# Two of eight maxima pairs per key strip through the score banks, reduced by VectorE in one instruction for both tiles

## The chip, the cores and the metric

The kernel runs on one core of a Trainium2 chip. The metric is the device time of one execution in microseconds; the times of a kernel are compared by the median of their runs. TensorE (PE) multiplies matrices into PSUM, which has eight banks of 128 partitions x 512 fp32; VectorE (DVE) and ScalarE (ACT) read them.

## The reference

Two transformer layers on 4,096 tokens of 256 features with 16 heads of 16. The first has block-sparse causal attention and an fp8 product. The second has two dense causal attentions over all 4,096 tokens, one with rotary positions and one with normalised queries and keys and a mixture of experts behind it. The dense attentions are what this case is about:

```
scores = jnp.einsum('bhqd,bhkd->bhqk', Q, K) / math.sqrt(Dh)
scores = jnp.where(causal, scores, jnp.finfo(scores.dtype).min)
attn = jax.nn.softmax(scores, axis=-1)
y = jnp.einsum('bhqk,bhkd->bhqd', attn, V)
```

## The kernel before

`attend` runs first for the sparse attention (stage "sparse") and then for both dense ones (stage "dense"). In the dense stage a unit is one strip j of 512 queries of a group of four heads; there are 2 attentions x 4 groups x 8 strips = 64 units. The strips go up from 0 to 7 in one group and down in the next. A unit has 4(j + 1) chunks of 128 keys, the last four of them on the diagonal, so that all have 1,152 chunks.

Softmax needs the maximum of each query over its keys before the exponentials. The kernel makes the scores twice. Ahead of time, with queries on the partitions, it makes a **tile** for each key strip kc, head h and block b of 128 queries: one product of 128 x 512 into one of three side banks (PSUM banks 5 to 7), of which VectorE takes the maximum into a column of `maxes`. That is 16 tiles per key strip, 4 per chunk, 4,608 in all. Tiles of the diagonal key strip (kc == j) are 128 to 512 columns wide and go through a masked reduction (L944), the others through a plain one (L951). When a unit's tiles are done VectorE negates the maxima ("negate"), TensorE transposes them ("hand", L818), and a DMA puts them into extra rows of the queries.

Later, with keys on the partitions, comes the **score**: for each chunk two pairs of products (L845), two heads into two neighbouring banks (pair 0 in banks 0 and 1, pair 1 in banks 2 and 3). ScalarE turns each pair into probabilities with one exp over 128 x 1,024 (L908), and the next user of the pair's banks waits for that exp. One chunk later TensorE **weighs** the values with them (L885, four heads side by side into bank 4; each product stands as two records in the trace). At a unit's end ScalarE copies bank 4 (L913), and in the second chunk of the next unit TensorE transposes the copy ("out", L823) into a side bank, and VectorE divides.

Heads with even and odd numbers use the upper and lower half of TensorE's rows, so that two such products run side by side. Only order on each engine and semaphores set the schedule. The order is written out in `order`: tiles go ahead of the scores by `lead(n)` chunks, and `emit_tiles(goal)` puts tiles into the order until their number reaches the goal. Before, a chunk reads on TensorE: two tiles, two score pairs, two tiles, the weighing of the chunk before. A side bank's next user waits for VectorE's reduction of the third tile back.

In short signs, used below: T a tile, S a score pair, W a weighing, "wide" the new pair.

## Time and profile before

| what | value |
| --- | --- |
| median of 3 runs | 5092.77 us (5092.59 to 5112.78) |
| span of the profiled execution | 5116.3 us |
| PE, DVE, ACT busy over the span | 4781.3, 4006.1, 2867.2 us |
| PE busy share over the span | 93% |
| dense stage | about 1179 to 4360 us |
| mean granted TensorE clock | 0.934 |

The profiled execution is one execution of its own, and its span lies just above the highest of the three runs; no time of its own is given beside the span. A group's busy time is the union of its instructions, and the ends of matmuls are modelled. Start times of matmuls are more telling than their lengths.

### The profile page before, as it was taken

The page shows a single profiled execution, that of the slowest core. Times are in us where ns is not written, and L with a number is a line of the kernel's source. Part 1 is how long each engine was busy: PE and PEld are TensorE (multiplying, and loading weights), DVE is VectorE, ACT ScalarE, POOL GpSimd, SP SyncE. Part 2 cuts the span into 40 slices and gives each one's busy share as a digit, 9 for nine tenths or more (in the row PEclk, how much of TensorE's full clock was granted, in tenths as well). Part 3 has the DMA queues.
Part 4 walks back from the last instruction along what each step waited for, and adds up shares of the span by engine and source line. Part 5 has one row for each costly group of instructions (what it writes and reads, how often), then busy time and mean ns, then how long its engine had stood idle before and what let it go on. Part 6 is the DMA issues. An engine that isn't in the chain of part 4 may idle for free.

```text
span 5116.3 us, 82733 instructions
## 1 busy us (share of the span) xinstructions
PE 4781.3 (93%) x31872; PEld 2539.4 (50%) x31872; DVE 4006.1 (78%) x9075; ACT 2867.2 (56%) x3349; POOL 241.8 (5%) x259
## 2 busy tenths in 40 slices
PE   6699997868999999999999999999999999899999
PEld 5455555754434344433334433334443333688888
DVE  8677775767898988888888989988899875555555
ACT  4356554433566766666666667666567677332232
POOL 5200001110000000000000000000000000300000
PEclk9799898877899999999999999999899999899999
DMA  6622223765000201200300300300300000210010
GB/s 192 175 77 69 65 51 105 230 221 97 16 11 14 48 16 32 43 9 5 50 13 21 58 9 5 50 13 20 54 11 8 9 7 7 71 42 21 21 42 9
DMA packets 259185, 258.36 MB, mean 50 GB/s; under 512 B 78288, under 2 KB 198096, under 8 KB 257440
## 3 DMA queue, kind: packets, MB, share of 16 engines
q1 hardware_dynamic: 250784, 212.86, 14.8%
q0 software_dynamic: 6240, 38.80, 4.7%
q8 instruction: 251, 4.11, 0.3%
q10 hardware_dynamic: 1768, 1.42, 0.2%
q14 instruction: 142, 1.16, 0.1%
HBM read 145.44 MB, written 105.97 MB: 49 GB/s over the span
## 4 chain that ended last, share of the span: by engine, by line
PE 73%; DVE 19%; issue 5%; ACT 2%; SPq 1%; DMA 1%; DVEq 0%; ACTq 0%
PE psum L885 24%; PE psum L813 20%; PE psum L76 14%; DVE maxes_dense L951 11%; PE psum L845 4%; PE psum L777 3%; PE psum L802 2%; PE psum L823 1%; PE psum L854 1%; PE psum L1656 1%; DVE masked_scores_dense L944 1%; PE psum L809 1%; PE psum L1636 0%; PE psum L864 0%; ACT probs_dense L908 0%
## 5 line engine op out<-in xcount | busy, mean ns | idle before, releaser
L908 ACT ACTIVATE probs_dense<-psum 128x1024 f32<-128x1024 f32 (+3 forms) x2304 | 2068.1, 950 | 1042.2 <-PE psum L845 755.1
L951 DVE TENSOR_REDUCE maxes_dense<-psum 128x1 f32<-128x512 f32 x3584 | 2227.5, 684 | 232.1 <-PE psum L813 231.3
L813 PE MATMUL psum<-keys,queries_dense 48*128 48x512 f32 (+3 forms) x4608 | 1553.0, 477 | 114.6 <-DVE maxes_dense L951 22.1
L813 PEld LDWEIGHTS psum<-keys,queries_dense 48*128 48x128 f32 x4608 | 668.2, 191 | 1471.4 <-DVE maxes_dense L951 1143.6
L885 PE MATMUL psum<-probs_dense,values 128*32 128x512 f32 (+3 forms) x9216 | 1181.2, 591 | 0.0
L845 PE MATMUL psum<-queries_dense,keys 50*128 50x512 f32 (+3 forms) x4608 | 809.7, 407 | 11.5 <-ACT probs_dense L908 11.2
L944 DVE CUSTOM_DVE_ANT_0 masked_scores_dense<-psum,causal_add 128x128 f32<-128x128 f32 (+3 forms) x1024 | 452.4, 488 | 151.5 <-PE psum L813 132.2
L845 PEld LDWEIGHTS psum<-queries_dense,keys 50*128 50x128 f32 x4608 | 449.6, 193 | 106.4 <-ACT probs_dense L908 60.0
L944 DVE CUSTOM_DVE_ANT_0 masked_scores_sparse<-psum,after_add 128x512 f32<-128x512 f32 x512 | 326.2, 687 | 99.9 <-PE psum L802 99.0
L1763 ACT ACTIVATE activated<-psum 128x512 f32<-128x512 f32 x208 | 124.4, 598 | 417.5 <-PE psum L76 405.8
L885 PEld LDWEIGHTS psum<-probs_dense,values 128*32 128x32 f32 x9216 | 189.9, 109 | 273.1 <-issue 203.0
L908 ACT ACTIVATE probs_sparse<-psum 128x1024 f32<-128x1024 f32 x224 | 217.7, 1022 | 147.2 <-PE psum L777 59.7
L802 PE MATMUL psum<-str_keys,queries_sparse 48*128 48x512 f32 x512 | 179.6, 513 | 48.3 <-DMA own_values<-v_scratch 25.8
L1898 DVE CAST hid_high<-activated 128x512 fp32r<-128x512 f32 x208 | 91.9, 442 | 143.5 <-ACT activated L1763 140.7
L1900 DVE TENSOR_TENSOR hid_low<-activated,hid_high 128x512 fp32r<-128x512 f32 x208 | 150.4, 723 | 7.2
L802 PEld LDWEIGHTS psum<-str_keys,queries_sparse 48*128 48x128 f32 x512 | 72.2, 195 | 168.2 <-DVE maxes_sparse L944 88.8
L885 PE MATMUL psum<-probs_sparse,str_values 128*32 128x512 f32 x1024 | 148.7, 655 | 0.0
L777 PE MATMUL psum<-tri_key,eye_bf 64*128 64x128 bf16 x2048 | 147.3, 223 | 0.0
L908 ACT ACTIVATE probs_sparse<-psum,after_bias 128x1024 f32<-128x1024 f32 x96 | 101.6, 1111 | 67.0 <-PE psum L854 67.0
L854 PE MATMUL psum<-queries_sparse,str_keys 50*128 50x512 f32 x512 | 127.3, 462 | 1.6 <-ACT probs_sparse L908 1.6
L948 DVE TENSOR_REDUCE maxes_sparse<-psum 128x4 f32<-128x512 f32 x128 | 83.7, 689 | 53.3 <-PE psum L809 51.7
L1912 DVE SCALAR_TENSOR_TENSOR xa_s<-psum,wts,xa_s 128x192 f32<-128x192 f32 x128 | 52.8, 416 | 81.6 <-PE psum L76 80.8
(296 smaller groups left out, 5252.6 us busy)
## 6 DMA issues: line engine op xcount, KB each, us to landing
v_scratch<-ve_s SPq DMA_DIRECT2D x96, 256.0 KB, 3.5
queries_dense<-parts_scratch SPq DMA_DIRECT2D x384, 64.0 KB
keys<-parts_scratch POOLq DMA_DIRECT2D x42, 512.0 KB, 18.0
parts_scratch<-part_high SPq DMA_DIRECT2D x16, 1024.0 KB, 4.3
parts_scratch<-part_low SPq DMA_DIRECT2D x16, 1024.0 KB, 7.1
values<-v_scratch POOLq DMA_DIRECT2D x8, 2048.0 KB, 35.3
queries_sparse<-parts_scratch SPq DMA_DIRECT2D x192, 64.0 KB
own_keys<-parts_scratch SPq DMA_DIRECT2D x192, 64.0 KB
```

The source lines that it names most:

```text
L76: m = pe.matmul(out_ap, left(l, c), right(r, c), start=(n == 0), stop=(n == len(pairs) - 1))
L777: m = pe.matmul(bank, eye2[own, part, :], addend, start=start and part == 0, stop=stop and part == 1)
L802: m = pe.matmul(bank, q[rows(h, TROWS), h // 2, b * P:(b + 1) * P], str_keys[n // STRIPS][rows(h, TROWS), h // 2, :], start=True, stop=True)
L813: m = pe.matmul(bank[:, 0:width], q[rows(h, TROWS), h // 2, b * P:(b + 1) * P], k[rows(h, TROWS), h // 2, kc * STRIP:kc * STRIP + width], ...
L845: m = pe.matmul(full[:, first_col:STRIP], k[own, h // 2, c * P:(c + 1) * P], q[own, h // 2, first_col:STRIP], start=True, stop=not diagonal)
L854: m = pe.matmul(full, str_keys[n // STRIPS][own, h // 2, c * P:(c + 1) * P], q[own, h // 2, :], start=True, stop=not partly)
L885: m = pe.matmul(psum[own_rows, 4, cols], vt, probs[(2 * m_at + h // 2) % 6][:, h % 2, cols], start=(c == 0), stop=(c == sizes[n] - 1 and b ...
L908: act.activation(probs[i % 6][:, :, first_col:STRIP], psum[:, at2:at2 + 2, first_col:STRIP], ACT.Exp, scale=SCALE, **extra).then_inc(exp_d ...
L944: m = dve.tensor_tensor_reduce(out=masked_scores[e % 2][:, 0:width], in0=bank[:, 0:width], in1=mask, scale=1.0, scalar=-3e38, op0=ALU.add, ...
L951: m = dve.tensor_reduce(mx[:, h * BLOCKS + b, kc:kc + 1], bank, AX.X, ALU.max)
L1763: act.activation(gs[k % 2][:], h_bank(u), func).then_inc(activated, 1)
L1900: dve.tensor_tensor(low[:, f, :], g[:], high[:, f, :].bitcast(F32), ALU.subtract).then_inc(hid_split, 1)
```

## The change

Of the eight pairs of tiles (even and odd head, same block of queries) that a full key strip has, the two of the last block of queries (b = 3, one for each pair of heads) no longer go to side banks. They become one **wide** pair: TensorE writes both tiles into the pair of score banks whose turn it is (L851 in the new kernel), and VectorE takes the maxima of both in one instruction over 128 x 2 x 512. So each key strip below the diagonal keeps 12 tiles and gets 2 wide pairs; the strip on the diagonal keeps 16 tiles. There are 448 wide pairs in place of 896 tiles.

Score pairs and wide pairs now take the two pair banks in turn, in the order in which they stand (`pair_users`, `wait_pair`). Each waits for the user two before it: for its exp if it was a score pair, for VectorE's wide reduction if it was a wide pair.

The tiles are spread over two chunks: an even chunk has S S T T W, an odd one T S wide T T T S W. Where there is no wide pair in the piece (the diagonal strip's tiles), the odd chunk has T S T T T T T S W. The leads are rounded to even numbers of chunks.

Counted in the new order, its 576 pairs of chunks are: 283 with a wide pair and nothing else, 60 with a wide pair in which the unit's own scores are on the diagonal, 33 more with a wide pair and a "hand", 50 with a wide pair at the start of a unit ("out"), 7 with a burst of tiles at a unit's end, 125 with tiles of the diagonal strip, 18 without tiles.

The core of the diff:

```diff
@@ -573,33 +573,44 @@
             if sparse:
                 return [("strided", 2 * i + odd, b) for i in range(PAIRS) for b in range(BLOCKS) for odd in range(2)] + [
                     ("local", odd, b) for b in range(0, BLOCKS, 2) for odd in range(2)]
-            return [(kc, 2 * i + odd, b) for kc in range(j + 1) for i in range(PAIRS) for b in range(BLOCKS) for odd in range(2)]
+            return [(kc, 2 * i + odd, b) for kc in range(j + 1) for i in range(PAIRS) for b in range(BLOCKS) for odd in range(2)
+                    if kc == j or b < BLOCKS - 1]
+
+        def steps_of(n):
+
+            steps = [("tile", n, tile) for tile in tiles_of(n)]
+            if sparse:
+                return steps
+            for kc in reversed(range(units[n][2])):
+                for i in reversed(range(PAIRS)):
+                    steps.insert(kc * GROUP * (BLOCKS - 1) + i * 2 * (BLOCKS - 1) + 3, ("wide", n, (kc, i, BLOCKS - 1)))
+            return steps
 
         def lead(n):
             if sparse:
                 return sizes[0] + 2
             if n >= len(units) - STRIPS:
                 return sizes[n] + 4
-            return min(max(sizes) + 4, 10 + int((2 * BLOCKS * (ends[n] - sizes[n])) ** 0.5))
+            return min(max(sizes) + 4, 2 * int(5 + (2 * BLOCKS * (ends[n] - sizes[n])) ** 0.5 / 2))
 
         order = []
-        ahead = [(n, t) for n in range(len(units)) for t in tiles_of(n)]
-        at = 0
+        ahead = [step for n in range(len(units)) for step in steps_of(n)]
+        at = made = 0
 
         def emit_tiles(goal):
-            nonlocal at
-            while at < min(goal, len(ahead)):
-                n, tile = ahead[at]
-                first_tile = at == 0 or ahead[at - 1][0] != n
-                if first_tile:
+            nonlocal at, made
+            while at < len(ahead) and made < goal:
+                kind, n, what = ahead[at]
+                if at == 0 or ahead[at - 1][1] != n:
                     order.append(("queries", n + 1, None))
-                order.append(("tile", n, tile))
-                of_unit = at - 4 * (ends[n] - sizes[n])
-                if of_unit == 5 and n >= 1:
+                order.append((kind, n, what))
+                before, made = made, made + (2 if kind == "wide" else 1)
+                of_unit = 4 * (ends[n] - sizes[n]) + 5
+                if before <= of_unit < made and n >= 1:
                     order.append(("hand", n - 1, None))
                 at += 1
-                if at == 4 * ends[n]:
+                if made == 4 * ends[n]:
                     order.append(("negate", n, None))
                     if n == len(units) - 1:
                         order.append(("hand", n, None))
@@ -610,17 +621,29 @@
             order.append(("unit", n, None))
             for c in range(sizes[n]):
                 m = ends[n] - sizes[n] + c
-                emit_tiles(4 * (m + lead(n)) + 2)
+                goals = [4 * (m + lead(n)) + more for more in (2, 2, 4)]
+                if not sparse:
+                    goals = [4 * (m - c % 2 + lead(n)) + more for more in ((0, 0, 2), (3, 8, 8))[c % 2]]
+                emit_tiles(goals[0])
                 for h in range(GROUP):
                     order.append(("score", n, (m, c, h)))
                     if n >= 1 and c == 1 and h == 3:
                         order.append(("out", n - 1, None))
                     if h % 2 == 1:
-                        emit_tiles(4 * (m + lead(n)) + (2, 4)[h // 2])
+                        emit_tiles(goals[1 + h // 2])
                 if c >= 1:
                     order.append(("weigh", n, (m - 1, c - 1)))
             order.append(("weigh", n, (m, c)))
         order.append(("out", len(units) - 1, None))
+
+        pair_users, wide_at = [], {}
+        for kind, n, what in order:
+            if kind == "wide":
+                wide_at[n, what] = len(wide_at)
+                pair_users.append(("reduced", wide_at[n, what] + 1))
+            elif kind == "score" and what[2] % 2 == 1:
+                pair_users.append(("exp_done", 2 * what[0] + what[2] // 2 + 1))
+        ring_at = {user: r for r, user in enumerate(pair_users)}
 
         side_at = {}
@@ -777,10 +801,16 @@
                             m = pe.matmul(bank, eye2[own, part, :], addend, start=start and part == 0, stop=stop and part == 1)
                     return m
 
+                def wait_pair(r):
+
+                    if r >= 2:
+                        name, count = pair_users[r - 2]
+                        pe.wait_ge(wide_reduced if name == "reduced" else exp_done, count)
+
                 if sparse:
                     pe.wait_ge(sparse_masks_in, SPARSE_MASKS)
                 for kind, n, what in order:
-                    if kind not in ("tile", "hand", "out", "unit", "score", "weigh"):
+                    if kind not in ("tile", "wide", "hand", "out", "unit", "score", "weigh"):
                         continue
                     a, g, j = units[n]
                     slot = n % held if sparse else n // STRIPS % 2
@@ -813,6 +843,14 @@
                             m = pe.matmul(bank[:, 0:width], q[rows(h, TROWS), h // 2, b * P:(b + 1) * P],
                                           k[rows(h, TROWS), h // 2, kc * STRIP:kc * STRIP + width], start=True, stop=True)
                         m.then_inc(side_filled, 1)
+                    elif kind == "wide":
+                        kc, i, b = what
+                        r = ring_at["reduced", wide_at[n, what] + 1]
+                        wait_pair(r)
+                        for odd in range(2):
+                            m = pe.matmul(psum[:, 2 * (r % 2) + odd, :], q[rows(odd, TROWS), i, b * P:(b + 1) * P],
+                                          k[rows(odd, TROWS), i, kc * STRIP:(kc + 1) * STRIP], start=True, stop=True)
+                        m.then_inc(wide_filled, 1)
                     elif kind == "hand":
                         pe.wait_ge(negated, past + n + 1)
                         pe.transpose(bank[0:MROWS * GROUP * BLOCKS, 0:P], neg_parts[n % 2][:].bitcast(F32).rearrange("p o s h b -> p (o s h b)"),
@@ -830,12 +868,11 @@
                             pe.wait_ge(masks_in, 16 * mask_loads)
                     elif kind == "score":
                         m_at, c, h = what
-                        i = 2 * m_at + h // 2
-                        at2 = 2 * (i % 2)
-                        if h % 2 == 0 and i >= 2:
-                            pe.wait_ge(exp_done, i - 1)
                         if h % 2 == 0:
                             continue
+                        r = ring_at["exp_done", 2 * m_at + h // 2 + 1]
+                        at2 = 2 * (r % 2)
+                        wait_pair(r)
                         pair = [psum[:, at2, :], psum[:, at2 + 1, :]]
                         if not sparse:
                             diagonal = c >= BLOCKS * j
@@ -950,9 +987,17 @@
                         else:
                             m = dve.tensor_reduce(mx[:, h * BLOCKS + b, kc:kc + 1], bank, AX.X, ALU.max)
                         m.then_inc(side_freed, 1)
+                    elif kind == "wide":
+                        kc, i, b = what
+                        at2 = 2 * (ring_at["reduced", wide_at[n, what] + 1] % 2)
+                        dve.wait_ge(wide_filled, wide_at[n, what] + 1)
+                        by_row = maxes[n % 2][:].rearrange("p (h o b) s -> p h o b s", o=2, b=BLOCKS)
+                        dve.tensor_reduce(by_row[:, i, :, b, kc], psum[:, at2:at2 + 2, :], AX.X, ALU.max).then_inc(wide_reduced, 1)
                     elif kind == "negate":
                         a, g, j = units[n]
                         mx, n3 = maxes[n % 2], neg_parts[n % 2]
+                        if wide_at and j >= 1:
+                            dve.wait_ge(wide_reduced, wide_at[n, (j - 1, PAIRS - 1, BLOCKS - 1)] + 1)
                         dve.wait_ge(side_freed, side_at["tile", n, tiles_of(n)[-1]] + 1)
                         if n >= 2:
                             dve.wait_ge(side_filled, side_at["hand", n - 2, None] + 1)
```

The rest gives the semaphores `wide_filled` and `wide_reduced`, the bank `at2` of ScalarE's exp by `ring_at`, and the stage's last waits.

What TensorE has in its row in the middle of a unit, before. The rows are one chunk, from the weighing of the chunk before to the next one (`keys,queries_dense` are tiles, `queries_dense,keys` scores, `probs_dense,values` weighings; x4 of scores is two pairs):

```order
L885 MATMUL psum<-probs_dense,values 32x512 x4
L813 MATMUL psum<-keys,queries_dense 128x512 x2
L845 MATMUL psum<-queries_dense,keys 128x512 x4
L813 MATMUL psum<-keys,queries_dense 128x512 x2
L885 MATMUL psum<-probs_dense,values 32x512 x4
```

The same place in the new kernel, two chunks (L843 is a tile, L882 a score, L922 a weighing, L851 the wide pair):

```order
L882 MATMUL psum<-queries_dense,keys 128x512 x4
L843 MATMUL psum<-keys,queries_dense 128x512 x2
L922 MATMUL psum<-probs_dense,values 32x512 x4
L843 MATMUL psum<-keys,queries_dense 128x512
L882 MATMUL psum<-queries_dense,keys 128x512 x2
L851 MATMUL psum<-keys,queries_dense 128x512 x2
L843 MATMUL psum<-keys,queries_dense 128x512 x3
L882 MATMUL psum<-queries_dense,keys 128x512 x2
L922 MATMUL psum<-probs_dense,values 32x512 x4
```

The odd chunk's two score pairs have moved apart, with the wide pair and three tiles between them, and in the even chunk nothing stands between the weighing and the scores.

The tiles of a diagonal strip on TensorE, before, two chunks:

```order
L813 MATMUL psum<-keys,queries_dense 128x128 x2
L845 MATMUL psum<-queries_dense,keys 128x512 x4
L813 MATMUL psum<-keys,queries_dense 128x256 x2
L885 MATMUL psum<-probs_dense,values 32x512 x4
L813 MATMUL psum<-keys,queries_dense 128x384 x2
L845 MATMUL psum<-queries_dense,keys 128x512 x4
L813 MATMUL psum<-keys,queries_dense 128x512 x2
L885 MATMUL psum<-probs_dense,values 32x512 x4
```

And now:

```order
L882 MATMUL psum<-queries_dense,keys 128x512 x4
L843 MATMUL psum<-keys,queries_dense 128x128 x2
L922 MATMUL psum<-probs_dense,values 32x512 x4
L843 MATMUL psum<-keys,queries_dense 128x256
L882 MATMUL psum<-queries_dense,keys 128x512 x2
L843 MATMUL psum<-keys,queries_dense 128x256
L843 MATMUL psum<-keys,queries_dense 128x384 x2
L843 MATMUL psum<-keys,queries_dense 128x512 x2
L882 MATMUL psum<-queries_dense,keys 128x512 x2
L922 MATMUL psum<-probs_dense,values 32x512 x4
```

Five tiles now stand in a row between the score pairs of the odd chunk. They were two and two.

The start of a unit on TensorE, before, from the last weighing of the unit ahead:

```order
L885 MATMUL psum<-probs_dense,values 32x128 x4
L813 MATMUL psum<-keys,queries_dense 128x512 x2
L845 MATMUL psum<-queries_dense,keys 128x512 x4
L813 MATMUL psum<-keys,queries_dense 128x512 x4
L845 MATMUL psum<-queries_dense,keys 128x512 x4
L823 MATMUL psum<-ident,outs_dense 128x128 x4
```

And now:

```order
L922 MATMUL psum<-probs_dense,values 32x128 x4
L882 MATMUL psum<-queries_dense,keys 128x512 x4
L843 MATMUL psum<-keys,queries_dense 128x512 x3
L882 MATMUL psum<-queries_dense,keys 128x512 x2
L851 MATMUL psum<-keys,queries_dense 128x512 x2
L843 MATMUL psum<-keys,queries_dense 128x512 x3
L882 MATMUL psum<-queries_dense,keys 128x512 x2
L861 MATMUL psum<-ident,outs_dense 128x128 x4
```

The wide pair and three tiles now stand ahead of the second chunk's last score pair and of the transposes.

## Rows read from the trace of the kernel before

**Rows 1.** Windows: busy us (instructions) of PE, PEld, DVE, ACT, POOL; clock; DMA.

```profile
1179.00:1600.00 421.00, 409.07 (x2373) 174.31 (x2371) 368.23 (x752) 231.16 (x260) 16.70 (x23) 0.86 0.15 29
1600.00:4360.00 2760.00, 2674.58 (x18369) 1099.88 (x18369) 2371.90 (x5191) 1873.43 (x2108) 31.87 (x46) 0.97 0.12 23
```

**Rows 2.** The chain that ended last, one steady chunk: start us, us, what.

```profile
3258.19 0.99 PE psum L885 x8
3259.19 0.47 PE psum L813 x2
3259.66 0.69 DVE maxes_dense L951
3260.35 0.04 issue
3260.39 0.50 PE psum L813
```

**Rows 3.** Timeline of DVE, steady chunk: start us, us, engine, line, operation [idle ahead].

```profile
3259.65 2.48 DVE L951 TENSOR_REDUCE maxes_dense<-psum 128x1 f32<-128x512 f32 x4 [0.21 <-PE psum L813]
```

**Rows 4.** Timeline of PE, the same chunk.

```profile
3259.12 0.49 PE L813 MATMUL psum<-keys,queries_dense 48*128 48x512 f32 x2
3259.45 0.64 PE L845 MATMUL psum<-queries_dense,keys 50*128 50x512 f32 x4
3259.93 0.97 PE L813 MATMUL psum<-keys,queries_dense 48*128 48x512 f32 x2
3260.82 1.07 PE L885 MATMUL psum<-probs_dense,values 128*32 128x512 f32 x8
```

**Rows 5.** Timeline of ACT, the same chunk.

```profile
3259.90 1.94 ACT L908 ACTIVATE probs_dense<-psum 128x1024 f32<-128x1024 f32 x2 [0.76 <-PE psum L845]
```

**Rows 6.** Groups of DVE by form, 1179 to 4360 us: busy, mean ns.

```profile
L944 DVE CUSTOM_DVE_ANT_0 masked_scores_dense<-psum,causal_add 128x512 f32<-128x512 f32 x250 | 162.3, 687 | 1.5 <-PE psum L813 1.1
L944 DVE CUSTOM_DVE_ANT_0 masked_scores_dense<-psum,causal_add 128x384 f32<-128x384 f32 x250 | 129.5, 555 | 77.9 <-PE psum L813 77.9
L944 DVE DVE_READ_ACCUMULATOR2_ANT maxes_dense<- 128x1 f32 x998 | 83.1, 83 | 0.0
```

**Rows 7.** Timeline of ACT over the tiles of a diagonal strip and a "hand".

```profile
3265.17 1.94 ACT L908 ACTIVATE probs_dense<-psum 128x1024 f32<-128x1024 f32 x2 [0.63 <-PE psum L845]
...
3269.71 4.02 ACT L908 ACTIVATE probs_dense<-psum 128x1024 f32<-128x1024 f32 x4 [0.51 <-PE psum L845]
3274.38 1.94 ACT L908 ACTIVATE probs_dense<-psum 128x1024 f32<-128x1024 f32 x2 [0.64 <-PE psum L845]
...
3280.71 1.94 ACT L908 ACTIVATE probs_dense<-psum 128x1024 f32<-128x1024 f32 x2 [0.96 <-PE psum L845]
```

**Rows 8.** Timeline of ACT at the start of a unit.

```profile
2595.19 0.60 ACT L913 ACTIVATE outs_dense<-psum 128x512 f32<-128x512 f32 x1 [1.24 <-PE psum L885]
2595.83 1.94 ACT L908 ACTIVATE probs_dense<-psum 128x1024 f32<-128x1024 f32 x2
2598.30 1.94 ACT L908 ACTIVATE probs_dense<-psum 128x1024 f32<-128x1024 f32 x2 [0.53 <-PE psum L845]
2601.52 1.02 ACT L908 ACTIVATE probs_dense<-psum 128x1024 f32<-128x1024 f32 x1 [1.28 <-PE psum L845]
```

**Rows 9.** Timeline of PE at the same start.

```profile
2598.43 0.66 PE L823 MATMUL psum<-ident,outs_dense 128*128 128x128 f32 x4
2599.75 1.06 PE L885 MATMUL psum<-probs_dense,values 128*32 128x512 f32 x8
```

**Rows 10.** Windows, behind another unit's start; the third column from the end is the clock.

```profile
2662.50:2666.50 4.00, 4.00 (x17) 1.62 (x17) 2.58 (x5) 1.38 (x3) 0.00 (x0) 0.50 0.36 82
```

**Rows 11.** Timeline of PE, same place.

```profile
2663.20 1.94 PE L885 MATMUL psum<-probs_dense,values 128*32 128x512 f32 x8
```

**Rows 12.** Timeline of ACT, same place.

```profile
2661.77 1.94 ACT L908 ACTIVATE probs_dense<-psum 128x1024 f32<-128x1024 f32 x2 [1.60 <-PE psum L845]
2666.33 1.94 ACT L908 ACTIVATE probs_dense<-psum 128x1024 f32<-128x1024 f32 x2 [2.62 <-PE psum L845]
```

More of the change, by code:

```diff
@@ L637, in attend @@
                 masks_in = sem("masks_in")
+                wide_filled, wide_reduced = sem("wide_filled"), sem("wide_reduced")
             side_filled, side_freed = sem(f"side_filled_{stage}"), sem(f"side_freed_{stage}")
@@ L903, in attend_act @@
                             i = 2 * m_at + half
-                            at2 = 2 * (i % 2)
+                            at2 = 2 * (ring_at["exp_done", i + 1] % 2)
                             act.wait_ge(scored, i + 1)
@@ L1016, in attend @@
                        (ao_stored[0], 16 * ((past + len(units)) // 2)), (ao_stored[1], 16 * ((past + len(units)) // 2)),
-                       (split_done, len(splits[2]))])
+                       (split_done, len(splits[2]))]
+                      + ([] if sparse else [(wide_reduced, len(wide_at))]))
     middle_early = ExitStack()
```

## The prediction

> **What bounds the kernel now.** I read first the windows: the dense stage runs from about 1179 to 4360 us, 62% of the span, with TensorE at 97%, VectorE at 86 to 87% and ScalarE at 55 to 68% of it [rows 1]. Neither share says which is the limit, since a matmul's end is modelled. So I read the chain that ended last in a steady stretch [rows 2]: a reduction of VectorE (0.69), 0.04 of issue, the tile that waited for its bank (0.50), the eight weighing records (0.99), two tiles (0.47), a reduction again. That is one chunk, 2.70 us. The reader should see that it is a loop between two engines over the three side banks, and that neither is full: in the timeline of the same chunk VectorE works 2.48 and then stands 0.21 waiting for a tile [rows 3], which TensorE could not bring while it weighed; TensorE stands between the third tile, 3259.93 [rows 4], and the fourth, 3260.39 [rows 2]: 0.46 where two scores or tiles side by side take 0.24. ScalarE has 0.76 of slack per chunk [rows 5].
>
> Units of cost, all start to start [rows 2 to 5, 8]: first tile pair behind a weighing 0.34; a score pair 0.24; a tile that had to wait, to the weighing behind it, 0.42; one that had not, about 0.10 less (0.34 less 0.24, the load of its weights), 0.31; weighing 1.00 (0.99 in the chain); tile to its reduction 0.53; score pair to its exp 0.45; exps 0.92 apart, each 1.02 long; reductions 0.60 apart (2.48 less 0.69, over 3), each 0.69 long. A freed bank reaches TensorE 0.04 to 0.05 later [rows 2].
>
> **What the change does to VectorE.** 896 tiles become 448 wide ones. No row has a reduction over 1,024 columns. The masked ones take 555 ns for 384 columns and 687 for 512, 132 ns per 128 [rows 6], so 512 more columns cost 0.53 and a wide one 0.60 + 0.53 = 1.13. Bounds: 1.07 (nothing fixed) and 1.20 (two whole ones). The saving in VectorE's own work is only 0.07 x 448 = 31 us; the rest must come from the 0.21 to 0.29 of idle per chunk. The floor of two chunks goes from 4.80 to 4.73, against 5.40 that they take.
>
> A rule of the Trainium skill bears on this. It says (Perfetto Trace Analysis, Optimizing Scalar/DVE Operations) that each VectorE instruction on PSUM pays about 125 ns and that grouping helps if the engine is saturated. By it the 448 saved instructions would be worth 56 us; the rows give 31, and show the engine idle 0.21 per chunk, so not saturated.
>
> **The plain cycle, laid out.** The score pairs and the wide pair share two pair banks in turn: S_a S_b, S_c wide S_d. So S_d uses the bank of S_c and can't start before exp c has ended. Before, a score pair had the other bank's exp between them. Behind S_d's wait stand the weighing and the next two score pairs, so ScalarE and the side tiles wait with it. Time 0 is the tile T3 behind a weighing. S_c 0.34, exp c 0.79 to 1.81; wide 0.58, T4 and T5 0.81, T6 when T3 is reduced (0.53 to 1.22), 1.27. S_d 1.86, having waited for exp c. Weighing 2.28 to 3.28. S_a, S_b 3.28 to 3.86 (0.34 + 0.24), T1 and T2, weighing 4.17 to 5.17. The cycle is **5.17 against 5.40**: 0.23 won, not 0.67, since the chain is now TensorE's order with one exp in it. VectorE needs 4.73 of the 5.17, so every price in the bounds of the wide reduction gives the same cycle. The program order has 283 such pairs of chunks: -65 us. 60 more, in which the unit's own scores are on the diagonal, have shorter exps but mask products on TensorE, and VectorE's 4.73 is near; I give them -0.1 each, -6.
>
> **Where the new spread costs.** (1) The tiles of the diagonal strip have no wide pair: one pair of chunks then holds S S T T W, T S T T T T T S W, five tiles in a row on three banks ahead of S_d. With T3 (256 columns) at 0: S_c 0.23, T3's reduction 0.43 to 0.86 (by the step of 132 ns a masked one over 256 takes 0.42, and about 0.35 from start to start, as a plain one has 0.09 of its length under the next), T4's to 1.21, T5's (384) to 1.68 [rows 6]. T8 needs T5's bank: 1.73. S_d 2.07, weighing 2.39 to 3.39, S_a, S_b and two narrow tiles to 4.11, weighing to **5.11**. Before, these tiles are the quick ones, two per bank wait: from the exps at 3259.90, 3265.17, 3269.71 and 3274.38 the three pairs of chunks round a unit's strip take 5.27, 4.54 and 4.67 [rows 5, 7]. After: 5.17 + 5.11 + 5.11. That is +0.91, of which -0.23 is counted already: +1.14 for each of some 62 units, **+71 us**.
> (2) The start of a unit (50 with a wide pair). 0 is the end of the last weighing. The copy, which waits for it, I put at 0.14; it takes 0.60: to 0.74, exp a 0.78 to 1.80 (0.64 behind the copy's start), exp b 1.70 to 2.72 [rows 8]. S_c waits for exp a, the wide pair for exp b: 2.77. VectorE's queue is in order: the wide reduction runs from about 3.3 to 4.43 and T4, T5, T6 stand behind it. The output's transposes need T4's bank, freed at 5.11: 5.16 to 5.75 (0.66 long [rows 9], of which I count 0.59 till the next can begin), weighing 5.83 to 6.83, next exp a 7.28. That is 6.5 from exp to exp against 2595.83 to 2601.52, 5.69, now [rows 8]: +0.8, **+40 us**.
> (3) The transposition of the maxima ("hand") takes a fourth side bank in one cycle: T6 then waits for T4, reduced behind the wide one at 2.95. S_d 3.34, weighing 3.66 instead of 2.28: 6.55 against 6.33 (3274.38 to 3280.71 [rows 7]): +0.2 in 33 cycles, +7.
> Sum at full clock: -65 - 6 + 71 + 40 + 7 = **+47 us**.
>
> **The clock.** From 1600 to 4360 the granted clock averages 0.97 [rows 1], so about 6% of 2,760 us is at the lower level, 1.2 GHz. A fall stands in the rows: at 2658 a unit begins, TensorE has little work, and from 2662.5 on the clock is 0.50 and the weighing is 1.94 long [rows 10, 11] instead of 1.07 [rows 4]. The chunk from 2661.77 takes 4.56 [rows 12] where the same one of the other unit, from 2598.30, takes 3.22 [rows 8], and one more weighing is longer by 0.9: about 2.3 us for one fall. At 2595 much the same pattern passed without a fall. The stretch without weighing there, from 0.14 ahead of the copy to 2599.75 [rows 8, 9], grows from 4.70 to 5.83 in my layout, so more of the 57 unit starts should fall, and some diagonal strips. I take 15 more falls, +35 us; bounds 0 and all of 57 + 62, +270. The Trainium skill says the same of direction (TensorE: Matmul & The Clock Gate, Part 1): idle gaps throttle the array to half, activity releases it.
>
> Against the profiled execution's own time, whose span is 5116.3 us, just above the highest of the runs (5112.8): +47 + 35 = +82. The median of the runs is 5092.8; I add the same to it: **5175 us**.
>
> **Rivals.**
> - A. Layout right, clock falls spread further, to most unit starts and many strips: some 50 to 60 more falls, +130, with +47: about 5260. For it: TensorE stands longer in one piece. Chance 0.18.
> - B. No difference that can be told (within 0.5%, 25 us): strips and starts cost half of what I laid out (+55 for +111), so that with -65 the sum is near 0: about 5095. Prior starts may be bound by the load of the queries, which the change leaves. Chance 0.13.
> - C. Faster. The wide pair works as a deeper buffer. Decisive is S_d's wait for exp c: if TensorE finds it done (were the tiles T4 to T6 later than 1.86, or the wide pair's backlog carried over), the cycle falls towards VectorE's 4.73 and 343 cycles win up to 0.67, -230 with starts and strips unchanged: 5092.8 - 230 + 118 = about 4980. A milder form, -0.23 and no loss in the strips since VectorE arrives there with no backlog, gives 5092.8 - 71 + 47 = 5069. Against both: exp c is 1.02 long and starts 0.45 after S_c, while the work between is 0.9. Chance 0.09.
> - The change does not do what it says: the wide reduction costs two whole ones. It moves the cycle by nothing (4.80 < 5.17), so it is inside the forecast.
> - My forecast, 5130 to 5230: chance 0.60.
>
> **Numbers.** Likeliest 5175. The range runs from the equal case to near A: 5090 to 5255, its price range being 0.05 of wake-up in some 450 cycles (20 us each way) and the falls. Faster by over 0.5%: 0.09; within: 0.13; slower: 0.78. Half a per cent is about what runs of this kernel can tell (they lie 20 us apart).
>
> **What the profile after would show.** Steady pairs of chunks of 5.17, with S_d waiting for ScalarE's exp each time, and VectorE idle about 0.4 in each; wide reductions 1.2 long; strips of 5.1; unit starts of 6.5 with the transposes waiting for VectorE; a lower mean clock from 1600 on. I am wrong if steady cycles are under 5.0 or the strips near 4.6, and the size is off if the clock's mean stays at 0.97.

## The result, and the profile after

| | before | after |
| --- | --- | --- |
| median | 5102.77 us (4 runs, 5092.59 to 5121.64) | 5253.32 us (4 runs, 5246.36 to 5275.36) |
| profiled execution: span, clock | 5116.3 us, 0.934 | 5244.5 us, 0.918 |
| dense stage in the trace | 3179.1 us | 3305.2 us |

The ratio is 1.0304, interval 1.0275 to 1.0334: slower by 150 us. Between the two profiled executions it is 128 us (that of before lies high among its runs, that of after is the fastest of its own), and the dense stage holds 126 of them. I had said 5175 us, as likeliest in a band of 5130 to 5230, and 5090 to 5255 as the whole range. The result lies outside the band and at the upper end of the range, and the loss is nearly twice the 82 us that I had added up.

The chain that ended last, from the page of the kernel before:

```profile
PE 73%; DVE 19%; issue 5%; ACT 2%; SPq 1%; DMA 1%; DVEq 0%; ACTq 0%
```

From the page of the kernel after: the span, the busy times, the chain that ended last, and the two groups of VectorE that matter.

```profile
span 5244.5 us, 82288 instructions
PE 4824.7 (92%) x31872; PEld 2502.8 (48%) x31872; DVE 3982.1 (76%) x8627; ACT 2911.2 (56%) x3349; POOL 240.9 (5%) x259
PE 72%; DVE 13%; ACT 8%; issue 5%; DMA 1%; SPq 1%; POOL 0%; DVEq 0%; ACTq 0%; POOLq 0%
L988 DVE TENSOR_REDUCE maxes_dense<-psum 128x1 f32<-128x512 f32 x2688 | 1720.7, 684 | 337.8 <-PE psum L843 279.0
L995 DVE TENSOR_REDUCE maxes_dense<-psum 128x2 f32<-128x1024 f32 x448 | 548.1, 1223 | 6.1 <-PE psum L851 5.2
```

VectorE's busy time fell by 24 us and its share of the chain from 19 to 13%, while ScalarE's rose from 2 to 8%: in the plain cycle, shown below, its exp has taken VectorE's place. A wide reduction is 1223 ns long, 0.54 more than a plain one of 684.

The windows that answer to [rows 1], then three short ones that are used below, at a unit's start (3378) and round a hand (3351 and 3354). The third column from the end is the clock.

```profile
1179.00:1600.00 421.00, 400.32 (x2363) 166.01 (x2361) 360.38 (x688) 235.95 (x258) 16.67 (x23) 0.83 0.15 29
1600.00:4485.00 2885.00, 2728.15 (x18358) 1072.32 (x18358) 2355.62 (x4813) 1911.11 (x2106) 31.88 (x46) 0.94 0.12 22
3378.00:3382.00 4.00, 3.64 (x16) 1.54 (x18) 2.19 (x5) 0.79 (x1) 0.00 (x0) 0.50 0.17 35
3351.00:3354.00 3.00, 2.80 (x16) 0.87 (x8) 2.86 (x4) 2.41 (x3) 0.00 (x0) 1.00 0.02 5
3354.00:3358.00 4.00, 3.15 (x15) 1.18 (x17) 2.18 (x5) 1.02 (x1) 0.00 (x0) 0.72 0.02 6
```

From 1600 us on the clock averages 0.94 over 2,885 us where it was 0.97 over 2,760. At one half for the low level that is 2 x 0.06 x 2,885 = 346 us at 1.2 GHz against 2 x 0.03 x 2,760 = 166.

**The plain cycle.** The chain through one pair of chunks, against [rows 2]: start, us, what.

```profile
3314.77 0.99 PE psum L922 x8
3315.77 0.43 PE psum L843
3316.20 0.26 PE psum L882
3316.46 0.02 issue
3316.48 1.03 ACT probs_dense L945
3317.51 0.04 issue
3317.56 0.50 PE psum L882 x2
3318.05 1.00 PE psum L922 x8
```

No reduction stands in it. The weighing, T3 and S_c lead to exp c; S_d starts 0.05 after that has ended, and the weighing follows it; behind the rows shown come S_a S_b, two tiles and the next weighing, with no wait between them. VectorE in the same stretch:

```profile
3313.43 3.50 DVE L988 TENSOR_REDUCE maxes_dense<-psum 128x1 f32<-128x512 f32 x5
3316.88 1.23 DVE L995 TENSOR_REDUCE maxes_dense<-psum 128x2 f32<-128x1024 f32 x1
3318.02 1.88 DVE L988 TENSOR_REDUCE maxes_dense<-psum 128x1 f32<-128x512 f32 x3
```

ScalarE in the same stretch, and then over a strip and the "hand" behind it (against [rows 5] and [rows 7]):

```profile
3314.35 1.94 ACT L945 ACTIVATE probs_dense<-psum 128x1024 f32<-128x1024 f32 x2 [0.41 <-PE psum L882]
3316.48 1.02 ACT L945 ACTIVATE probs_dense<-psum 128x1024 f32<-128x1024 f32 x1 [0.20 <-PE psum L882]
3318.10 1.02 ACT L945 ACTIVATE probs_dense<-psum 128x1024 f32<-128x1024 f32 x1 [0.59 <-PE psum L882]
3319.52 1.02 ACT L945 ACTIVATE probs_dense<-psum 128x1024 f32<-128x1024 f32 x1 [0.40 <-PE psum L882]
...
3340.23 2.87 ACT L945 ACTIVATE probs_dense<-psum 128x1024 f32<-128x1024 f32 x3 [0.40 <-PE psum L882]
...
3345.34 2.86 ACT L945 ACTIVATE probs_dense<-psum 128x1024 f32<-128x1024 f32 x3 [0.41 <-PE psum L882]
...
3350.45 1.94 ACT L945 ACTIVATE probs_dense<-psum 128x1024 f32<-128x1024 f32 x2 [0.41 <-PE psum L882]
...
3358.02 1.94 ACT L945 ACTIVATE probs_dense<-psum 128x1024 f32<-128x1024 f32 x2 [1.38 <-PE psum L882]
```

3314.35 to 3319.52 is a cycle of 5.17. The two pairs of chunks of the strip take 5.11 each (3340.23, 3345.34, 3350.45); before, they were the quick ones, 4.54 and 4.67. The hand's cycle, from 3350.45, takes 7.57. TensorE in it:

```profile
3353.30 0.50 PE L843 MATMUL psum<-keys,queries_dense 48*128 48x512 f32 x1
3354.85 0.50 PE L843 MATMUL psum<-keys,queries_dense 48*128 48x512 f32 x1 [1.05 <-DVE maxes_dense L988]
...
3355.51 1.74 PE L922 MATMUL psum<-probs_dense,values 128*32 128x512 f32 x8
```

T6 waits for the bank for 1.05, as laid out, and the weighing behind it is 1.74 long instead of 1.06: the clock has fallen (1.00 up to 3354, 0.72 behind). Hand cycles that no stretch of low clock touches take 6.61; this one pays 0.96 for the fall. I had written nothing of that: I had the wait and not its price. TensorE at a start, against [rows 9]:

```profile
3375.91 0.54 PE L851 MATMUL psum<-keys,queries_dense 48*128 48x512 f32 x2 [0.41 <-ACT probs_dense L945]
...
3378.36 1.11 PE L861 MATMUL psum<-ident,outs_dense 128*128 128x128 f32 x4 [0.64 <-DVE maxes_dense L988]
3379.41 1.94 PE L922 MATMUL psum<-probs_dense,values 128*32 128x512 f32 x8
```

The wide pair waits for ScalarE, the transposes for VectorE, and by then the clock is at one half: 1.11 for what took 0.66, 1.94 for 1.06.

**All pieces, sorted.** I sorted the pairs of chunks of both traces by kind and took those that no stretch of low clock touches, us from exp to exp:

| kind (number) | before | forecast | after |
| --- | --- | --- | --- |
| plain (283) | 5.40 | 5.17 | 5.18 |
| two pairs of chunks of a strip (62) | 4.54, 4.67 | 5.11, 5.11 | 5.11, 5.11 |
| own scores on the diagonal (35; 25) | 4.98; 5.28 | -0.1 each | 4.70; 5.35 |
| hand (33) | 6.30 | 6.55 | 6.61 |
| start (32) | 5.69 | 6.5 | 6.53 (two untouched) |
| start with a hand in it (15) | 6.50 | none | none untouched; 7.3 in x4_hold |

The other three of the 50 starts have the own diagonal in them as well (5.58 before, 6.55 after). Two hands of the seven that stand in such a piece are untouched too, at 6.88.

The trace's record of the clock has 35 stretches at 1.2 GHz in the dense stage before (290 us together) and 80 after (440 us). By the piece in which they begin:

| stretches begin in | before | after |
| --- | --- | --- |
| the 47 starts with a wide pair (32 and 15 of the table) | 20 | 38 |
| the 33 hands | 0 | 27 |
| all others | 15 | 15 |

The 15 others after are six in the bursts at a unit's end, five in pieces without tiles, three in strips with a hand and one in a start on the own diagonal; none is in a plain cycle or in a strip without a hand. So the 45 more are 18 in starts and 27 in hands (x3 below, with the same order, has 34 in starts, 27 in hands and 13 others). What TensorE did before them: in the hands its longest stand (by the trace's modelled ends) was 0.05 to 0.51 us before and is 1.03 to 1.23 now; in the strips without a hand, where none begins, it is 0.22 at most.

Each piece put at the length of untouched pieces with the same order makes 3,094 us at full clock before, and 85 us of excess at the low clock; after, about 3,150 and 155 (with 7.3 for a start with a hand). So the 126 are **some 56 at full clock and some 70 of clock**; the pieces with bursts are never untouched and leave this open by a few us. Of the 70, 33 to 35 lie in the starts, 28 in the hands and 6 in plain cycles, into which a stretch runs on. At full clock the starts cost 42 (with 7.3 again), the hands 13, strips and plain cycles together 5, and the pieces on the own diagonal give 8 back.

### The profile page after: what moved, and what is told of

It reads as the page before. It is cut to its first block, busy times and chain, and to the rows that moved or that the text cites. A ratio compares the mean times of both kernels' runs of the same rounds, so it can differ in the third digit from the quotient of the medians.

```text
span 5244.5 us, 82288 instructions
## 1 busy us (share of the span) xinstructions
PE 4824.7 (92%) x31872; PEld 2502.8 (48%) x31872; DVE 3982.1 (76%) x8627; ACT 2911.2 (56%) x3349; POOL 240.9 (5%) x259
## 3 DMA queue, kind: packets, MB, share of 16 engines
q14 instruction: 138, 1.13, 0.1%
## 4 chain that ended last, share of the span: by engine, by line
PE 72%; DVE 13%; ACT 8%; issue 5%; DMA 1%; SPq 1%; POOL 0%; DVEq 0%; ACTq 0%; POOLq 0%
PE psum L922 24%; PE psum L76 14%; PE psum L882 12%; PE psum L843 10%; ACT probs_dense L945 7%; DVE maxes_dense L988 5%; PE psum L801 3%; PE psum L832 2%; DVE maxes_dense L995 2%; PE psum L861 2%; PE psum L891 1%; PE psum L1702 1%; PE psum L839 1%; PE psum L851 1%; PE psum L1682 0%
## 5 line engine op out<-in xcount | busy, mean ns | idle before, releaser
L945 ACT ACTIVATE probs_dense<-psum 128x1024 f32<-128x1024 f32 (+3 forms) x2304 | 2116.5, 952 | 1162.6 <-PE psum L882 817.7
L988 DVE TENSOR_REDUCE maxes_dense<-psum 128x1 f32<-128x512 f32 x2688 | 1720.7, 684 | 337.8 <-PE psum L843 279.0
L843 PE MATMUL psum<-keys,queries_dense 48*128 48x512 f32 (+3 forms) x3712 | 1198.0, 441 | 109.0 <-DVE maxes_dense L988 66.6
L882 PE MATMUL psum<-queries_dense,keys 50*128 50x512 f32 (+3 forms) x4608 | 1189.4, 462 | 56.8 <-ACT probs_dense L945 21.6
L922 PE MATMUL psum<-probs_dense,values 128*32 128x512 f32 (+3 forms) x9216 | 1218.8, 606 | 0.0
L843 PEld LDWEIGHTS psum<-keys,queries_dense 48*128 48x128 f32 x3712 | 555.9, 195 | 849.0 <-DVE maxes_dense L988 580.5
L882 PEld LDWEIGHTS psum<-queries_dense,keys 50*128 50x128 f32 x4608 | 520.2, 195 | 692.4 <-issue 249.8
L995 DVE TENSOR_REDUCE maxes_dense<-psum 128x2 f32<-128x1024 f32 x448 | 548.1, 1223 | 6.1 <-PE psum L851 5.2
L922 PEld LDWEIGHTS psum<-probs_dense,values 128*32 128x32 f32 x9216 | 186.8, 111 | 325.3 <-issue 284.0
L851 PE MATMUL psum<-keys,queries_dense 48*128 48x512 f32 x896 | 256.3, 496 | 17.7 <-ACT probs_dense L945 17.7
L801 PE MATMUL psum<-tri_key,eye_bf 64*128 64x128 bf16 x2048 | 196.0, 227 | 0.0
L851 PEld LDWEIGHTS psum<-keys,queries_dense 48*128 48x128 f32 x896 | 110.1, 190 | 125.2 <-ACT probs_dense L945 120.8
L922 PE MATMUL psum<-probs_sparse,str_values 128*32 128x512 f32 x1024 | 149.4, 658 | 0.0
```

The source lines that it names most:

```text
L801: m = pe.matmul(bank, eye2[own, part, :], addend, start=start and part == 0, stop=stop and part == 1)
L843: m = pe.matmul(bank[:, 0:width], q[rows(h, TROWS), h // 2, b * P:(b + 1) * P], k[rows(h, TROWS), h // 2, kc * STRIP:kc * STRIP + width], ...
L851: m = pe.matmul(psum[:, 2 * (r % 2) + odd, :], q[rows(odd, TROWS), i, b * P:(b + 1) * P], k[rows(odd, TROWS), i, kc * STRIP:(kc + 1) * STR ...
L882: m = pe.matmul(full[:, first_col:STRIP], k[own, h // 2, c * P:(c + 1) * P], q[own, h // 2, first_col:STRIP], start=True, stop=not diagonal)
L922: m = pe.matmul(psum[own_rows, 4, cols], vt, probs[(2 * m_at + h // 2) % 6][:, h % 2, cols], start=(c == 0), stop=(c == sizes[n] - 1 and b ...
L945: act.activation(probs[i % 6][:, :, first_col:STRIP], psum[:, at2:at2 + 2, first_col:STRIP], ACT.Exp, scale=SCALE, **extra).then_inc(exp_d ...
```

## The experiments

Medians; ratios are to the kernel before on the same chip. The kernel before had medians of 5107.33 (x1 to x4, 13 runs), 5102.82 (x5 to x8, 27 runs) and 5097.62 (x9, one run). The kernel after has its own 4 runs alone, so differences to it carry the few us by which these medians differ; x3, x2 and x9 are single runs.

| | time | ratio, interval |
| --- | --- | --- |
| x1_strips | 5202.5 (4 runs) | 1.017 [1.0124, 1.0216] |
| x2_spread_only | 5822.16 (1) | |
| x3_two_reductions | 5254.3 (1) | |
| x4_hold | 5158.0 (10) | 1.0097 [1.0064, 1.0129] |
| x5_plain_only | 5076.92 (10) | 0.9949 [0.9927, 0.997] |
| x6_before_hold | 5095.98 (10) | 0.9982 [0.9958, 1.0006] |
| x7_no_start_hand | 5154.77 (4) | 1.0102 [1.0069, 1.0135] |
| x8_plain_hold | 5077.23 (12) | 0.9949 [0.9929, 0.997] |
| x9_longer_exp | 5387.11 (1) | |

### The strips: the old spread where there is no wide pair

```diff
-                if not sparse:
+                if not sparse and wide_in(4 * (m - c % 2 + lead(n))):
                     goals = [4 * (m - c % 2 + lead(n)) + more for more in ((0, 0, 2), (3, 8, 8))[c % 2]]
```

> The changed kernel, but where the tiles of a diagonal strip stand (no wide pair in the piece) a chunk has again two tiles, two score pairs, two tiles. Theory L (the layout of the prediction: the strips cost at full clock, the rest is falls of the clock at unit starts and hands): each strip's two pairs of chunks go from 5.11 back to about 4.6, 45 to 70 us less than the changed kernel, and the number of stretches at 1.2 GHz (80 in its dense stage) stays. Rival G (the whole loss lies in the plain cycle and the starts, strips are hidden): within 15 us of the changed kernel.

5202.5, 51 us less than after. ScalarE over a strip in x1_strips:

```profile
3307.62 1.94 ACT L952 ACTIVATE probs_dense<-psum 128x1024 f32<-128x1024 f32 x2 [0.40 <-PE psum L889]
...
3313.27 1.94 ACT L952 ACTIVATE probs_dense<-psum 128x1024 f32<-128x1024 f32 x2 [0.88 <-PE psum L889]
...
3317.92 1.94 ACT L952 ACTIVATE probs_dense<-psum 128x1024 f32<-128x1024 f32 x2 [0.51 <-PE psum L889]
...
3322.34 1.94 ACT L952 ACTIVATE probs_dense<-psum 128x1024 f32<-128x1024 f32 x2 [0.40 <-PE psum L889]
```

5.65, 4.65 and 4.42 in place of 5.18, 5.11 and 5.11: 0.68 less, 42 us over 62 units, and the dense stage is 43 us shorter in the trace (3262.4 us). The stretches of low clock are 74, but x3 below, in which the order is that of after, has 74 too, so 6 fewer is scatter, as expected. The passage from a wide cycle into the old spread costs 0.47 of its own. So the strips' term was right.

### The spread alone: no wide pair, all 4,608 tiles in side banks

```diff
-                    if kc == j or b < BLOCKS - 1]
+                    ]
...
-            if sparse:
-                return steps
+            return steps
```

> The changed kernel without wide pairs: all 4,608 tiles through the side banks, spread over two chunks as in the change (S S T T W, T S T T T T T S W). Theory L: five tiles in a row on three banks, the pair of chunks takes about 6.0 us, about 250 to 300 us slower than the changed kernel; so the wide pairs are what makes the spread bearable, and the spread is the cost. Rival W (the wide pair is the cost, by its place in the score banks and the exp that the last score pair waits for): this kernel lies between the kernel before and the changed one.

The untouched plain cycle is 6.07 on average, as laid out, but the time is 5822, 569 more than after and about twice the loss that I expected. The dense stage of x2_spread_only, and one stretch of it:

```profile
1600.00:5055.00 3455.00, 3226.83 (x18599) 1241.05 (x18599) 2411.36 (x5264) 1946.13 (x2135) 33.72 (x48) 0.86 0.10 19
2605.00:2653.00 48.00, 44.36 (x232) 15.75 (x230) 34.75 (x56) 27.94 (x29) 0.00 (x0) 0.88 0.00 1
```

The clock is at 0.88 in the middle of a unit, where nothing but plain cycles stands, and ScalarE's starts there, 2605.81, 2612.23, 2619.37, 2625.81, 2632.91, are 6.42, 7.14, 6.44 and 7.10 apart: it falls within the steady cycle. There are 196 stretches, 1,116 us, of which 123 begin in plain cycles, and 223 of the 283 plain cycles are touched. The layout of the cycle is confirmed; my total had no term for the clock in it. So the spread alone is a large loss, and the wide pairs win most of it back.

### The price of the wide reduction: two of 128 x 512 in its place

```diff
-                        dve.tensor_reduce(by_row[:, i, :, b, kc], psum[:, at2:at2 + 2, :], AX.X, ALU.max).then_inc(wide_reduced, 1)
+                        for odd in range(2):
+                            m = dve.tensor_reduce(by_row[:, i, odd:odd + 1, b, kc], psum[:, at2 + odd:at2 + odd + 1, :], AX.X, ALU.max)
+                        m.then_inc(wide_reduced, 1)
```

> The changed kernel, each wide pair reduced by two instructions of 128 x 512 instead of one of 128 x 1024. Theory L: VectorE needs 4.80 instead of 4.73 of a cycle of 5.17, so the cycle stays and the time is within 15 us of the changed kernel. Rival V (VectorE still bounds the cycle): 0.07 x 448 = 30 us slower.

5254.3: no change (one run). The group in x3_two_reductions that stands for the wide ones:

```profile
L996 DVE TENSOR_REDUCE maxes_dense<-psum 128x1 f32<-128x512 f32 x892 | 572.9, 684 | 5.6 <-PE psum L851 5.1
```

27 us more of VectorE's work (572.9 for 545.7 to 548.1) cost nothing. "In one instruction for both tiles" is worth nothing that this run can tell; whatever the change wins in the plain cycle comes from where the tiles are put.

### What the low clock costs: TensorE kept busy where it stood

```diff
+                            for again in range(repeat.get((n, what), 1)):
-                                m = pe.matmul(bank[:, 0:width], ...
```

Tile products at unit starts are issued 3 times and beside a hand 4 times, with the same values into the same bank.

> The changed kernel with products of tiles at unit starts done three times and beside a hand four times (each time the same values into the same bank), so that TensorE is busy where it only waited. No work of the other engines changes. Theory F (45 more stretches at 1.2 GHz than before cost some 75 of the 128 us by which the two profiled executions differ): the stretches fall from 80 to 30 or fewer, and the time by 60 to 90 us. Rival G (TensorE would wait there anyway, the clock costs nothing): unchanged, or slower by the added products, some 10 to 30 us.

5158.0, 95 us less than after, with more work on TensorE. The dense stage from 1600 on in x4_hold:

```profile
1600.00:4398.00 2798.00, 2705.85 (x19032) 1130.71 (x19028) 2359.03 (x4816) 1912.39 (x2107) 31.86 (x46) 0.98 0.12 23
```

A start, TensorE in x4_hold:

```profile
3326.39 0.66 PE L874 MATMUL psum<-ident,outs_dense 128*128 128x128 f32 x4 [0.86 <-DVE maxes_dense L1001]
3326.97 1.06 PE L935 MATMUL psum<-probs_dense,values 128*32 128x512 f32 x8
```

The transposes still wait for VectorE, but take 0.66 and the weighing 1.06: full clock. 80 stretches became 24, 440 us at 1.2 GHz became 164. 95 us over 56 fewer stretches is 1.7 us each. In a hand the stand is filled; TensorE in one of x4_hold, against 3353.30 above:

```profile
3303.48 1.36 PE L856 MATMUL psum<-keys,queries_dense 48*128 48x512 f32 x5
3304.49 0.59 PE L895 MATMUL psum<-queries_dense,keys 50*128 50x512 f32 x2
3305.01 1.07 PE L935 MATMUL psum<-probs_dense,values 128*32 128x512 f32 x8
```

One hand of 33 begins a stretch now, where 27 did. This is the test of cause: order and semaphores are the same, and the untouched pieces got no shorter (plain 5.18, hand 6.62 for 6.61, start 6.64 for 6.53). By the sorted pieces the excess at the low clock falls by some 96 us and full clock grows by 8. The 96 are more than the 70 that the change had added, since stretches that the kernel before had are among them. The starts with a hand are held least: 12 of 15 still begin a stretch.

### Starts and hands without a wide pair

Strips keep the new spread; pieces with an "out" or a "hand" get tiles in side banks and the old spread (the core of the edit; `wides` and `wide_from` hold the pieces that keep a wide pair):

```diff
-                    if kc == j or b < BLOCKS - 1]
+                    if kc == j or b < BLOCKS - 1 or (n, kc, i) not in wides]
...
-                if not sparse:
+                if 4 * (m - c % 2 + lead(n)) in wide_from or not sparse and 4 * (m - c % 2 + lead(n)) in strip_from:
```

> The changed kernel, but the first pair of chunks of a unit and every piece with a hand have the old spread and no wide pair (343 wide pairs less those in pieces that a burst moves stay); strips stay spread as in the change. Theory F: two terms go, the longer starts and hands at full clock (some 45 us) and with them most of the 45 added stretches at 1.2 GHz (75 us): 90 to 120 us less than the changed kernel, with 35 to 45 stretches. Rival G (only the full-clock terms count): 30 to 50 us less, the number of stretches going down without a further gain.

5154.77, 99 us less than after. 48 stretches, 32 fewer than after: none begins in a hand (27 did), but the starts still have 33 (38 did; 20 in the kernel before, whose starts have the same spread). By the sorted pieces full clock gives about 45. The medians leave 53 for the clock, 1.65 us a stretch; the two profiled executions, whose dense stages differ by 78, leave 33, or 1.0.

### Wide pairs in plain pieces alone

The edit of the run before without `strip_from`, so that strips have the old spread too, and with `range(2, sizes[n] - BLOCKS, 2)` for the pieces, so that those on the own diagonal have it as well.

> Wide pairs and the new spread only in the 283 plain pairs of chunks; starts, hands, strips and the pieces whose own scores are on the diagonal as in the kernel before. Theory L and F: only the gain of 0.22 per plain cycle is left, less about 0.35 at each of some 50 passages from the new to the old spread, 65 - 20 = 45 us faster than the kernel before, at best 5055. Rival: the passages and a shifted lead eat the gain, no difference within 0.5%.

5076.92, ratio 0.9949 [0.9927, 0.997]: 26 us faster than before and 176 faster than after; with x8 the fastest version here. It has 35 stretches, as many as before. It keeps the leads rounded to even numbers, so these are not what costs the change its time. It wins less than I expected since each passage from a wide piece into an old one costs: among the untouched ones 5.65 to 5.79 in 50 places and 5.9 in 20, instead of 5.18, some 40 us together.

### The same products repeated in the kernel before, and in x5

> The kernel before with the same repeated products at starts and hands. Theory F: a clock stretch costs about the same in this kernel, so its 35 stretches go down to about 10 and its time by 30 to 50 us, to about 5055. If so, a saved stretch is worth 1.2 to 1.9 us. Rival G: no change or slower.

5095.98, ratio 0.9982 [0.9958, 1.0006]. The clock from 1600 on:

```profile
1600.00:4340.00 2740.00, 2678.24 (x18943) 1168.74 (x18939) 2386.19 (x5204) 1878.63 (x2110) 31.86 (x46) 1.00 0.12 23
```

35 stretches became 12 and the excess 37 us instead of 85. But the pieces at full clock grew from 3,094 to 3,125 us: the last piece of a unit from 4.98 to 5.42, a start with a hand from 6.50 to 6.55 and up to 6.67. The products that hold the clock now delay the work behind them; 7 us are left, which can't be told from nothing. Between the two kernels with repeated products, x4 and this one, 62 of the 150 us remain. That fits a clock part of well over half, but is no measure of it, since the products delay the two by different amounts (8 and 31 us).

> The kernel of x5_plain_only with repeated products of tiles at unit starts (three times) and beside a hand (four times). Theory F: the stretches at 1.2 GHz that the kernel before has at its own starts (some 28 of its 35) go too, another 30 to 50 us less than x5_plain_only, about 5010 to 5025. Rival: the added products delay the first tiles of a start and eat it: the same as x5_plain_only.

5077.23, the same as x5: 15 stretches instead of 35, and the gain eaten (the last piece of a unit is again 5.42, for 4.95 in x5). Here the rival was right.

### Is exp c in the chain: half an exp more ahead of it

```diff
+                            if not sparse and half == 0 and c % 2 == 1 and c < BLOCKS * j:
+                                act.activation(outs[n % 2][:].rearrange("p (o n) -> p o n", o=2), psum[:, at2:at2 + 2, 0:STRIP // 2], ACT.Exp, scale=SCALE)
```

An additional exp over 128 x 512, whose result nobody uses, stands ahead of exp c.

> The changed kernel with half an exp more (128 x 512 of the same pair, about 0.49 us, result not used) ahead of exp c, the first exp of each odd chunk off the diagonal. Theory L (exp c stands in the chain of the plain cycle: S_c, exp c, S_d, weighing): each plain pair of chunks goes from 5.18 to 5.67, strips by about 0.15, starts and hands not at all, since there the last score pair waits for VectorE or has slack: about 140 to 160 us slower than the changed kernel. ScalarE has 5.18 - 3.68 = 1.5 us of slack in a cycle, so rival V (the plain cycle is bounded by TensorE's own work, by VectorE or by the side banks, and S_d's wait is only where the slack shows) expects 0 to 20 us.

5387.11, 134 us more than after. The chain of x9_longer_exp through exp c:

```profile
3412.64 0.43 PE psum L843
3413.07 0.26 PE psum L882
3413.32 0.02 issue
3413.35 0.60 ACT outs_dense L946
3413.95 0.92 ACT probs_dense L947
3414.87 0.04 issue
3414.91 0.49 PE psum L882 x2
```

The plain cycle is 5.65 to 5.68 (+0.49, the added exp to the start of exp c), although ScalarE's gaps add up to 1.19 us per cycle in the kernel after (0.20 + 0.59 + 0.40). Strips (5.11), hands (6.61) and starts (6.53) did not move, so exp c is not in their chain; for the strips I had expected 0.15.

## Why the prediction was wrong

The direction and the layout at full clock were right (+56 for +47). What failed is the clock's term, the sentence "I take 15 more falls, +35 us": it measured some 70 us, because it looked for falls at unit starts and strips and put the hands at none.

- **Plain cycle.** 5.17 forecast, 5.18 measured, S_d waiting for exp c each time (chain, x9). The gain of 0.22 in 283 pieces is real; x5 is what remains of it after the passages. Rival C needed TensorE to find exp c done, and it never did. "VectorE idle about 0.4 in each" shows as no gap in the trace: its five reductions in a row take 3.50, where starts 0.60 apart would make 3.09, so the 0.4 lies between their starts; x3 shows that the slack is there.
- **Wide reduction.** 1223 ns long, against about 1.2, and 1.14 from its start to the next (3316.88 to 3318.02), against 1.13. Its price did not matter: x3 doubles the instructions and changes nothing. The Trainium skill (Perfetto Trace Analysis, Optimizing Scalar/DVE Operations) puts about 125 ns on each VectorE instruction on PSUM; the estimate from it for 448 saved instructions is 56 us. The trace shows 24 us less busy time, and x3 shows none of it in the time. The Trainium skill says in the same place that grouping can help if the engine is saturated; here it is not, with 4.73 of work in a cycle of 5.18.
- **Strips.** 5.11 forecast and measured; x1 gets 0.68 of the 0.91 per unit back, and its passage costs 0.47 of its own.
- **Own diagonal.** -0.28 x 35 and +0.07 x 25: -8 us, forecast -6.
- **Hands** at full clock: 6.61 against 6.55, and 6.88 for the seven on the own diagonal: 13 us for 7. **Starts**: 6.53 against 6.5; I had no term for the 15 starts that hold a hand too (7.3 against 6.50), but at 0.8 they cost what I had given each of the 50. Starts come to 42 us, forecast 40.
- **Clock, the failed step.** 45 more stretches and not 15. For the starts I was near: 18 more, 33 to 35 us. The hands I had left out: I had laid out that T6 waits for T4 there, and TensorE does stand 1.05 us, but the term for it, +0.2 each, was at full clock. 27 of 33 hands now begin a stretch, where none did: 28 us, and 6 more in the plain cycles behind. The strips, which I had feared, have none; TensorE stands 0.22 at most in them. The added stretches cost 70 / 45 = 1.6 us each by the sorted pieces, 1.7 by x4 and 1.0 to 1.65 by x7, less than my 2.3 (the 35 of before cost 85 / 35 = 2.4). So the count was three times too low and the price 1.4 times too high. x4 shows that it is the clock and not the order.
- **Rival A** is nearest in mechanism and in number, with 50 to 60 falls where there are 45; but it put them in many strips, and its own sum, 5092.8 + 130 + 47, is 5270 and not 5260. That 5260 lies so near the result is partly luck: its price per fall is too high, and the base is 10 us too low.
- **Base.** The 78 us between 5175 and 5253 are three things: 10 since I added to 5092.8, where the 4 runs give 5102.8; 22 since the execution profiled before lies 15 us high among its runs and that of after 7 us low; and 46 of forecast, 9 at full clock, 35 of clock and 2 outside the dense stage.

What is not settled: why one start keeps the clock and the next, with the same order, loses it, and why the starts of x7, which have the spread of before, have 33 stretches where before has 20.

## What to carry to other kernels

Lay out the repeating cycle from start times, and find the wait that the new sharing of a bank creates: here a wide buffer took VectorE out of the chain and put an exp into it, which left 0.22 of the 0.67 us that VectorE's slack allowed. Count the irregular places (diagonal, unit start, transposition) with the same care, since here they outweigh 283 good cycles. The new order paid only where the pattern is plain, and every passage between two patterns had a price. At each place where a layout makes TensorE stand longer than before, as in the hands here (1.05 us for 0.5 at most), add a term for the clock beside the wait itself, and test it by repeating products there.

## What the runs showed of the hardware

- The clock can fall in a steady cycle, not only at breaks: in x2, whose plain cycles take 6.07 at full clock, 123 stretches at 1.2 GHz begin in them; over one stretch of 48 us the mean is 0.88, and the 223 touched cycles take 7.00 on average.
- Stands of 1.03 to 1.23 us inside a hand went with a fall in 27 of 33 places; with 0.05 to 0.51 (before) none had one, and with the stand filled (x4) one had. Strips, with 0.22 at most, had none.
- Repeated products hold the clock (80 stretches to 24, 35 to 12, 35 to 15), for -95, -7 and 0 us of time: the products also delay the work behind them.
